# Cross-attention and gated FFN on one core: FFN tile by tile, squares turned through DRAM, and read-back trips cut by rows

## The reference

```
n1 = layernorm(x)
sim = (n1 Wq)(ctx Wk)^T * scale          # 154 scores per head and row
sim = (sim - mean) * 1.5 + mean;  p = softmax(sim)
x  = x + p (ctx Wv) Wout + bout

n2 = layernorm(x);  prev = n2 shifted by one row, zeros at a batch's start
xk = mu_k*n2 + (1-mu_k)*prev;  xr = mu_r*n2 + (1-mu_r)*prev
x  = x + sigmoid(xr W_r^T) * (relu(xk W_k^T)^2 W_v^T)
```

## Time and profile before

| | |
|---|---|
| median of 3 runs | 743.82 us (743.12 to 744.17) |
| profiled execution | 744.54 us, its span 742.7 us |
| PE busy | 736.4 us (99%), TensorE clock granted 1.0 throughout |
| DVE, ACT, POOL busy | 516.0, 426.8, 123.7 us |
| DMA | 106.52 MB, mean busy share of the 16 engines 47.6% on SP's queue |
| first loop step (scores of tile 6) begins | 128.81 us |

### The profile page before, as it was taken

One profiled execution on the slowest core, in us unless ns is written; L12 is line 12 of the kernel. 1 busy time (PEld: TensorE's weight loads), 2 busy tenths in 40 slices (PEclk: granted clock), 3 DMA queues, 4 the chain that ended last, 5 costly groups with the idle time before them and its releaser, 6 DMA issues.

```text
span 742.7 us, 13556 instructions
## 1 busy us (share of the span) xinstructions
PE 736.4 (99%) x3948; PEld 643.0 (87%) x3948; DVE 516.0 (69%) x1085; ACT 426.8 (57%) x1204; POOL 123.7 (17%) x279
## 2 busy tenths in 40 slices
PE   9999999999999999999999999999999999999998
PEld 8957888888988888898888889888888988888887
DVE  3678987777667766666776766677666667766662
ACT  3568865575746556564655656465665646565332
POOL 1111111202121120212112021211202121120211
PEclk9999999999999999999999999999999999999999
DMA  9966643545444353545435354543535454343301
GB/s 330 252 152 172 202 136 115 148 147 177 140 146 147 117 164 87 176 142 167 129 109 159 93 175 144 163 126 115 167 84 175 143 167 128 109 156 93 112 28 43
DMA packets 87239, 106.52 MB, mean 143 GB/s; under 512 B 9999, under 2 KB 64169, under 8 KB 87211
## 3 DMA queue, kind: packets, MB, share of 16 engines
q1 hardware_dynamic: 87172, 106.15, 47.6%
q10 hardware_dynamic: 39, 0.04, 0.0%
HBM read 58.70 MB, written 47.45 MB: 143 GB/s over the span
## 4 chain that ended last, share of the span: by engine, by line
PE 90%; SPq 5%; DVE 1%; DMA 1%; ACT 1%; issue 1%; POOL 0%; POOLq 0%; DVEq 0%
PE ffn L494 12%; PE ffn L496 12%; PE ffn L495 12%; PE scores L495 9%; PE scores L496 9%; PE scores L494 9%; PE attended L496 9%; PE attended L495 9%; PE attended L494 9%; SPq L353 3%; SPq L336 1%; PE attended L544 1%; PE attended L543 1%; DMA x_rows<-normed 1%; SPq L333 1%
## 5 line engine op out<-in xcount | busy, mean ns | idle before, releaser
L494 PE MATMUL scores<-A_hi,xT_hi 128*128 128x462 f32 x372 | 129.9, 349 | 0.8 <-DVE B_lo L973 0.8
L495 PE MATMUL scores<-A_lo,xT_hi 128*128 128x462 f32 x372 | 130.4, 351 | 0.0
L496 PE MATMUL scores<-A_hi,xT_lo 128*128 128x462 f32 x372 | 130.0, 349 | 0.0
L775 ACT ACTIVATE probs<-scores,neg_max 128x154 f32<-128x154 f32 x248 | 93.2, 387 | 46.7 <-DVE neg_max L1033 46.6
L496 PE MATMUL attended<-B_hi,pT_lo 128*128 128x512 f32 x288 | 112.5, 391 | 0.0
L495 PE MATMUL attended<-B_lo,pT_hi 128*128 128x512 f32 x288 | 112.4, 390 | 0.0
L494 PE MATMUL attended<-B_hi,pT_hi 128*128 128x512 f32 x288 | 112.1, 389 | 0.0
L1033 DVE TENSOR_REDUCE neg_max<-scores 128x3 f32<-128x462 f32 (+1 forms) x93 | 53.3, 581 | 80.9 <-PE scores L496 80.9
L1334 POOL TENSOR_SCALAR var<-stats 128x1 f32<-128x1 f32 x64 | 13.2, 206 | 462.4 <-DVE stats L979 461.3
L494 PEld LDWEIGHTS scores<-A_hi,xT_hi 128*128 128x128 f32 x372 | 70.2, 189 | 8.0 <-issue 1.7
L495 PEld LDWEIGHTS scores<-A_lo,xT_hi 128*128 128x128 f32 x372 | 70.1, 188 | 5.6
(11 more groups left out here) (171 smaller groups left out, 1583.3 us busy)
## 6 DMA issues: line engine op xcount, KB each, us to landing
prob_rows<-probs SPq DMA_DIRECT2D x32, 704.0 KB, 4.1
probs_handed<-prob_rows SPq DMA_DIRECT2D x128, 176.0 KB, 3.4
x_rows<-normed SPq DMA_DIRECT2D x61, 256.0 KB, 2.4
handed<-x_rows SPq DMA_DIRECT2D x244, 64.0 KB, 1.9
x_in<-in_x SPq DMA_DIRECT2D x32, 256.0 KB, 3.0
out<-x SPq DMA_DIRECT2D x31, 256.0 KB, 3.7
wq<-in_L_xattn_Wq SPq DMA_DIRECT2D x2, 1024.0 KB, 10.6
wout<-in_L_xattn_Wout SPq DMA_DIRECT2D x1, 2048.0 KB, 20.1
```

What stands on the lines that cost most here:

```text
L494: te.matmul(psum, left[0], right[0], start=first, stop=False)
L495: te.matmul(psum, left[0], right[1], start=False, stop=False)
L496: return te.matmul(psum, left[1], right[0], start=False, stop=last)
L775: last = nc.scalar.activation(probs[:, q, cols], score_banks(t)[b][:, (h - h0) * J:(h - h0 + 1) * J], ACT.Exp, bias=neg_max[:, h:h + 1], a ...
```

## The change

1. The FFN goes tile by tile. `key_rows` replaces `key_columns`: `xk` is the left operand, the weights move, 512 columns a matmul, and rows come out on the partitions. Per tile PE now does keys, gate and, one tile behind, the values.
2. The squares are then not transposed: they are stored to a new DRAM tensor (`store_squares`, 256 KB a tile), read back by four DMAs (`hand_squares`, buffer `act_handed`), turned by DVE (`squares_turn`) and split. SP issues 22 DMAs a step in place of 17. The last tile's squares are turned by PE.
3. All read-back trips (`x`, `x2`, probabilities, squares) are cut otherwise: each of the four DMAs takes 32 rows, all columns, and writes all 128 partitions; in the source the four column quarters are now the outermost dimension, 32 rows the next. The same 512-byte (1408-byte) pieces reach the same places.
4. The order of DVE, ACT and POOL is rewritten around it, the start is longer by hand, `W_v` is loaded after `wq` is done with, and one `delta` buffer serves.

```diff
-                rows = dram[bass.ds(t * P, P), :].rearrange("(r i) (q k) -> q i r k", i=Q, q=4)
-                for q in range(4):
-                    sp.dma_start(handed[q * Q:(q + 1) * Q, :].rearrange("i (r k) -> i r k", r=4), rows[q]
-                                 ).then_inc(landed, 16)
+            def hand(dram, t, landed, to=handed):
+                for r in range(4):
+                    rows = dram[bass.ds(t * P + r * Q, Q), :].rearrange("i (q k) -> q i k", q=4)
+                    sp.dma_start(to[:, r * P:(r + 1) * P], rows).then_inc(landed, 16)
...
-                rows = p_dram[bass.ds(t * P, P), :].rearrange("(r i) (q k) -> q i r k", i=Q, q=4)
-                for q in range(4):
-                    sp.dma_start(probs_handed[q * Q:(q + 1) * Q, :, :], rows[q]).then_inc(probs_landed, 16)
+                for r in range(4):
+                    rows = p_dram[bass.ds(t * P + r * Q, Q), :].rearrange("i (q k) -> q i k", q=4)
+                    sp.dma_start(probs_handed[:, r, :], rows).then_inc(probs_landed, 16)
...
+            def store_squares(t):
+                sp.wait_ge(square_ready, t + 1)
+                sp.dma_start(act_dram[bass.ds(t * P, P), :], act[:]).then_inc(act_stored, 16)
+            def hand_squares(t):
+                sp.wait_ge(act_stored, 16 * (t + 1))
+                if begun(t - 1):
+                    sp.wait_ge(act_turned, t)
+                hand(act_dram, t, act_landed, act_handed)
...
+                if is_tile(t - 1) and not is_last(t - 1):
+                    store_squares(t - 1)
                 if is_tile(t) and not is_last(t):
                     store_x2(t)
+                if is_tile(t - 1) and not is_last(t - 1):
+                    hand_squares(t - 1)
                 if is_tile(t) and not is_last(t):
                     hand_x2(t)
...
-            def key_columns(q):
-                te.wait_ge(mixed_split["k"], 2 * q + 2)
-                for j in range(2):
-                    if begun(q - 1):
-                        te.wait_ge(gated, 2 * q + j - 1)
-                    for m in (2 * j, 2 * j + 1):
-                        for c in range(DC):
-                            cols = tuple(w[:, c, m * P:(m + 1) * P] for w in WT["k"])
-                            last = three_passes(T[1 + j][:, (m % 2) * 2 * P:(m % 2 + 1) * 2 * P], cols,
-                                                (mixed_hi["k"][:, c, :], mixed_lo["k"][:, c, :]),
-                                                c == 0, c == DC - 1)
+            def key_rows(t):
+                if begun(t - 1):
+                    te.wait_ge(relu_ready, t)
+                te.wait_ge(mixed_split["k"], t + 1)
+                ffn_rows(T[1], (mixed_hi["k"], mixed_lo["k"]), WT["k"]).then_inc(k_done, 1)
...
-                if is_pair(q) and half == 0:
-                    gate_rows(q, 0)
-                    key_columns(q)
-                if is_pair(q) and half == 1:
-                    gate_rows(q, 1)
-                    value_rows(q, 0)
+                key_rows(t - 1)
+                gate_rows(t - 1, turn_last_x2 if is_last(t) else None)
+                if not is_last(t + 1):
+                    value_rows(t - 2)
...
+            def squares_turn(t):
+                dve.wait_ge(act_landed, 64 * (t + 1))
+                if begun(t - 1):
+                    dve.wait_ge(kv_done, t)
+                turn_blocks(actT[:], act_handed[:], DC).then_inc(act_turned, 1)
```

More of the change, by code:

```diff
@@ L478, in _ @@
             load_x(5, 1)
+            hand_x(5)
             store_x2(1)
+            hand_probs(3)
             hand_x2(1)
-            hand_probs(3)
-            hand_x(5)
+            load_x(6, 2)
+            store_probs(4)
+            store_squares(0)
+            store_x2(2)
+            hand_probs(4)
+            hand_squares(0)
+            hand_x2(2)
+            store_x(6)
+            store_squares(1)
+            hand_x(6)
+            hand_squares(1)
+            store_probs(5)
+            load_x(7, 3)
+            hand_probs(5)
+            store_x2(3)
+            store(0, 0)
+            hand_x2(3)
+            store_squares(2)
+            hand_squares(2)
             turns(sp, step)
-            store(PAIRS - 1, 0, 2)
+            store(TILES - 2, 2)
             store_last()
@@ L732, in _ @@
             attend(1)
+            scores(4)
+            attend(2)
+            key_rows(0)
+            gate_rows(0)
+            scores(5)
+            key_rows(1)
+            gate_rows(1)
+            attend(3)
+            value_rows(0)
+            key_rows(2)
+            gate_rows(2)
+            value_rows(1)
             turns(te, step)
@@ new lines, in squares @@
+            def squares(t):
+                act_e.wait_ge(k_done, t + 1)
+                if is_last(t):
+                    act_e.wait_ge(xn_stored, 16 * (TILES - 2))
+                if begun(t - 1):
+                    act_e.wait_ge(act_stored, 16 * t)
+                nc.scalar.activation(act[:], T[1][:], ACT.Relu).then_inc(relu_ready, 1)
+                act_e.wait_ge(relu_ready, t + 1)
+                to, rows = (in_quarters(normed), by_quarter(act)) if is_last(t) else (act[:], act[:])
+                nc.scalar.activation(to, rows, ACT.Square).then_inc(square_ready, 1)
@@ L872, in step @@
                     pack_hi(t + 2)
-                if is_pair(q):
-                    open_gate(q, half, t)
-                if is_tile(t):
+                if is_last(t):
+                    x2_norm(t, s)
+                if is_last(t) or is_last(t - 1):
+                    squares_hi(t - 2)
+                squares(t - 1)
+                if is_tile(t) and not is_last(t):
                     x2_norm(t, s)
@@ L963, in _ @@
                 probs_hi(3, i)
-            squares(0, 0)
-            turns(act_e, step, from_second=True)
+            mixed_high("k", 1)
+            open_gate(0, 0)
+            mixed_high("r", 1)
+            x_norm(6, 2)
+            for b in range(2):
+                exponentials(5, b)
+            squares_hi(0)
+            exponentials(5, 2)
+            normalise_early(5)
+            squares(1)
+            x_hi(6)
+            pack_hi(5)
+            mixed_high("k", 2)
+            open_gate(1, 1)
+            mixed_high("r", 2)
+            squares_hi(1)
+            x2_norm(3, 3)
+            for i in range(3):
+                probs_hi(4, i)
+            squares(2)
+            open_gate(2, 0)
+            turns(act_e, step)
         @block.vector
@@ L1093, in mix @@
+            def mix(w, t):
+                dve.wait_ge(delta_ready, t + 1)
+                if begun(t - 1):
+                    dve.wait_ge(r_done if w == "r" else k_done, t)
                 for c in range(DC):
-                    last = v.scalar_tensor_tensor(out=mixed[w][:, c, before], in0=change[:, c, :],
-                                                  scalar=mu[w][:, c:c + 1], in1=xn2T[:, c, before],
-                                                  op0=ALU.mult, op1=ALU.add)
+                    last = v.scalar_tensor_tensor(out=mixed[w][:, c, :], in0=delta[:, c, :], scalar=mu[w][:, c:c + 1],
+                                                  in1=xn2T[:, c, 0:P], op0=ALU.mult, op1=ALU.add)
```

408 lines of the change are left out of this document (211 added, 197 removed).

## The result

The changed kernel takes **1048.51 us** (median of 6 runs, 1045.75 to 1051.74), the kernel before beside it 743.99 us (743.12 to 744.53, 6 runs): 1.409 times as long, 95% interval 1.4064 to 1.4123. Forecast were 994 us and a range of 805 to 1121. The profiled execution took 1049.8 us, its span is 1048.0.

What follows compares the result with a forecast made beforehand. Four DMA engines carrying every read-back, in a serial cycle through SP and DVE, make a step 29.9 us against PE's 21.65: 744.54 + 239 (29 x 8.25) + 10 for the last tiles = 994 us, range 805 to 1121.

Steps and rivals of the forecast that it cites:

- the forecast's own range: Whole kernel: 965 (29 x 7.35 + 10) to 1121 us (29 x 12.65 + 10), around 994, chance 0.64.
- What bounds the kernel, and PE's own gain: Loop before the change: matmuls back to back, 21.65 us a step; the new keys take 5.1 us off PE's work.
- The 68 us: Key matmuls: the gain that listed durations suggest (217 against 149 us), called not real because those durations overlap.
- Four engines: Read-backs: outermost DRAM count 4 puts all on the same four DMA engines, 24.4 us of load a tile each.
- The probabilities' 8.0 us: Probabilities' read-back: load on each of the four engines per tile, with bounds 7.1 and 12.4 us.
- The circle: Loop: SP's stores, landings and read-backs and DVE's turn to add_x run in series, 29.9 us a tile.
- Start and tail: Outside the loop: 8.25 us excess for each of tiles 2 to 5; last three tiles add about 10 (0 to 20).
- Rival (a): Loop: four engines but no serial part, rings stay full, 24.4 us a tile, 836 us; chance 0.17.
- Rival (b): Read-backs: 16 engines kept or load spread, PE without gaps, 740.4 us, faster by 0.5%; chance 0.13.
- The 0.13 for faster: Whole kernel: chance given to a result faster by over 0.2% (1.5 us).
- Rival (c): SP's queue: 16 engines, but the wait for stored squares and 22 issues delay trips, 0.7 us a step, 760; chance 0.03.
- The signs to look for: Profile after: PE share about 70%, probability read-backs landing near 8 us or more, mean DMA share 0.35 to 0.45.

Runs made afterwards that it cites:

- experiment 3: Changed kernel with each read-back's 32 rows outermost in the source and column quarters inside, still onto 128 partitions, data order wrong: 757.51 us, 1.018 of before.
- experiment 1: Changed kernel with all read-backs cut by column quarters again, as before the change: 761.71 us, 1.022 of the kernel before.
- experiment 4: Changed kernel with each read-back of x, x2 and squares as eight DMAs of two column quarters, outermost 2: 1293.19 us.
- experiment 7: Changed kernel with only DVE's and ACT's order changed: add_x and the probabilities' late scaling and low part ahead of the turn of x: 934.28 us.
- experiment 9: Experiment 8's kernel with x2 read back ahead of the squares and the start's order changed on SP and DVE: 749.6 us, 1.0072 of before.
- experiment 10: Experiment 9's kernel with the read-back of tile 1's squares directly behind its store, and DVE's order to match: 745.31 us, 1.0017 of before.
- experiment 8: Experiment 1's kernel with experiment 7's order of DVE and ACT added: 753.08 us, 1.0115 of before.

## Why the prediction was right, and where not

The 1048.51 us lie inside the forecast's own range (965 to 1121), 5.5% above its 994.

- **What bounds the kernel, and PE's own gain.** Right. A step is 21.48 us of matmuls without gaps, before 21.65; 0.17 x 32 is 5.4 against the 5.1 worked out from the starts. The 68 us that the durations pretend never showed.
- **Four engines.** Right, by the packets to the last one, the quarter share in the isolated trip (3.6 us of data, forecast 3.7), and experiment 3, which differs from after only in what is outermost in the source; experiment 1 differs in the partitions too. That it is always the same four is shown by the share between 485.76 and 503.21, a quarter while twelve DMAs stand in the rings, and by experiment 4 for a trip by itself. The probabilities' 8.0 us were taken from a line through two sizes and are near: that window holds 82.1 engine-us; less two trips of 14.9 and two stores of 11.1, 30.1 are left, an estimate of 7.5 us on each of the four (7.8 with the trips at the 14.3 measured now).
- **The circle.** Right in kind: experiment 7 broke it by order alone and gained 4.34 us a step. The size fell short: 29.9 forecast, 31.6 measured. In its own pieces, issue to issue: turn of `x` to load 2.9, measured 3.1; load to the squares' read-back 4.55, measured 5.45 (480.31 to 485.76); three read-backs and the store of `x` 17.45, measured 17.45 (485.76 to 503.21), an agreement to the digit that is luck in part, since the probabilities in it were less than 8.0; read-back of `x` to its turn 5.05, measured 5.49. What was sized too small are the two pieces with stores or a read-back out of an idle queue. Here 1.0 and 1.4 us pass between the issue and the first data, which the forecast had only in part (1.35 for landing and next start together). In the first piece the store of `x2` also runs before the squares' has landed, where the forecast let it fall into the 1.35s: from 480.31 to 486.00 the 16 engines were busy for 65 engine-us, 4.1 us each, where load, probabilities and squares were to take 3.2.

```profile
q1 hardware_dynamic: 576, 1.51, 71.7%
```

The 1.65 us in 25 steps are 42 of the 56 us by which the profiled execution (1049.8) lies above 994. The lower end of the forecast's own range is a slip: 744.54 + 29 x 7.35 + 10 gives 968, not 965; nothing hangs on it.
- **Start and tail.** 33 us for tiles 2 to 5, measured 35.9, and that is luck: experiment 1, without the new cut, is already 11.8 us late there, for which the forecast had nothing, so the cut's own part is about 24. The tail was taken at 10 (0 to 20) and was 21.0, just outside its bound and 11 above its value. It was a guess from shorter PE work; that the last trips are chained no less, with less PE work to hide them, is an argument, not tested.
- **Rival (a)**, 836, rings without gaps: experiment 7 shows what cutting DVE out of the circle gives, 27.25 a step. 24.4 was not reached by any kernel here.
- **Rival (b)**, 740, was priced wrong although it didn't come. Experiment 1 is that case: 761.7, not faster but 2.2% slower. The mechanism, PE going on without a gap, held in the loop nearly (21.86 against 21.48), while start and tail were taken at nothing. Experiments 9 and 10 show one late read-back stopping PE for 4.6 us at the start. The 0.13 for faster rested on this price and should have been near nothing.
- **Rival (c)** had 760 from SP's queue with 16 engines; experiment 1 lands there. But experiment 8's order, without fewer SP issues, takes 8.6 of its 17.7 us over before away, and experiment 10, with the same 22 issues a step, is 1.4 us above before. So all but 1.4 of the 17.7 us went by the order of the instructions, and that 760 came near was luck.
- **The signs to look for.** PE's share came to 78%, not 70, since PE after a wait is slow and so counts as busy. The landing of the new read-backs can't be read, the page has none for them; what stands behind them, the store of `x`, landed in 8.7 us. The DMA share of 34.6% is just under the low edge given, 0.35.

## What to carry to other kernels

Count the completions of a DMA in the packets before trusting its shape: here an outermost dimension of 4 or 2 on the DRAM side put all of it on that many engines, and the mean DMA share fell while the kernel became DMA-bound. A trip's cost is then not its data but the circle it lies in; write the circle issue to issue (store, landing, read-back, turn, the instruction that the next issue waits for) and reorder the one engine that closes it before anything else. And when PE runs without gaps, price the start and the tail of a new order by themselves: in the loop the tile-by-tile FFN was 3 us better, and all of it was given back outside.

## What the runs showed that was not expected

- Four DMAs of a read-back are issued by SP mostly in 1.8 to 1.9 us with 16 engines each and in 2.5 to 2.9 with 4, and eight of two engines in 5.0 to 5.7: 0.44 to 0.48, 0.63 to 0.71 and 0.62 to 0.71 us each. Single ones stray (2.40 with 16 engines in experiment 9). Why fewer engines make the issue longer is open.
- After a wait of 6.84 us the first key matmul lasted 0.77 us and the next ones 0.63, against 0.39 at the full clock; a wait costs more than its own length. In experiment 10 the matmuls take 734.1 us in all, after the change 812.6, with the same 3568.
- With 16 engines in both, the read-backs onto 128 partitions (experiment 3) were 4.2 us of 762 faster than those onto 32 (experiment 1). The order of the source differs too, so which of the two gave it is open.
